# Softmax over heads: GpSimd adds the two halves of the heads in two of five units

## The reference, cut to what matters

```python
q = (Query @ Wq.T).reshape(b, -1, H, DK).transpose(0, 2, 1, 3)
k = (Key @ Wk.T).reshape(b, -1, H, DK).transpose(0, 2, 1, 3)
v = (Value @ Wv.T).reshape(b, -1, H, DK).transpose(0, 2, 1, 3)
scores = jnp.einsum('bhqd,bhkd->bhqk', q, k) / jnp.sqrt(jnp.float32(DK))
attn = jax.nn.softmax(scores, axis=1)
ctx = jnp.einsum('bhqk,bhkd->bhqd', attn, v)
ctx = ctx.transpose(0, 2, 1, 3).reshape(b, -1, H * DK)
return ctx @ Wo.T
```

## Time and profile before

| | |
|---|---|
| time, median of 3 runs | 1636.36 us (1632.52 to 1644.97) |
| the profiled execution, its own time | 1630.4 us |
| its span, first to last instruction | 1628.7 us |
| mean granted TensorE clock | 0.916 of full speed |
| busy: PE, DVE, ACT, POOL | 1406.0, 987.6, 687.7, 628.2 us |

### The profile page before, as it was taken

How to read it: one execution, slowest core, us unless ns; L and a number is a source line. 1 busy time by engine, 2 the same in 40 slices (tenths; PEclk the granted TensorE clock), 3 DMA queues, 4 the chain that set the end, 5 groups by cost and what they waited for, 6 DMA issues and landing times. The chain is left out here.

```text
span 1628.7 us, 23696 instructions
## 1 busy us (share of the span) xinstructions
PE 1406.0 (86%) x9145; PEld 715.1 (44%) x9145; DVE 987.6 (61%) x1770; ACT 687.7 (42%) x1204; POOL 628.2 (39%) x626
## 2 busy tenths in 40 slices
PE   7868786988989999899868999899999877889984
PEld 3345443433334444444334444454445433355542
DVE  4898939777742211468566773745556344588866
ACT  2444432766742000257534774244434432355522
POOL 2487734354223221333124312533421312356762
PEclk8889997989999999879987998999999978999996
DMA  5000010000020000100001002000000010000000
GB/s 111 0 1 0 1 48 1 1 1 1 1 82 1 1 0 0 53 1 1 11 0 54 2 2 47 1 2 1 2 1 2 2 31 1 7 1 2 2 1 28
DMA packets 17382, 20.65 MB, mean 13 GB/s; under 512 B 7835, under 2 KB 13195, under 8 KB 16760
## 3 DMA queue, kind: packets, MB, share of 16 engines
q1 hardware_dynamic: 15440, 17.33, 3.6%
q10 hardware_dynamic: 1832, 1.80, 0.5%
HBM read 17.94 MB, written 1.05 MB: 12 GB/s over the span
## 5 line engine op out<-in xcount | busy, mean ns | idle before, releaser
L1852 DVE CUSTOM_DVE_ANT_0 P<-P,L2f_mask 128x128 f32<-128x128 f32 (+3 forms) x256 | 118.5, 521 | 99.9 <-PE P L1744 99.9
L1029 DVE TENSOR_REDUCE L0f_nm<-P 128x2 f32<-128x768 f32 (+3 forms) x88 | 97.5, 1120 | 38.1 <-PE P L926 37.9
L2028 PE MATMUL P<-L0m_hm,L0m_w 128*128 128x512 f32 x256 | 112.2, 597 | 0.0
L1822 ACT ACTIVATE L2f_prob<-P 128x1024 f32<-128x1024 f32 x80 | 80.6, 1025 | 73.1 <-PE P L1756 73.1
L1663 POOL TENSOR_SCALAR_AFFINE_SELECT L2f_prob<-L2f_prob 128x512 f32<-128x512 f32 x64 | 39.9, 638 | 161.4 <-ACT L2f_prob L1822 161.4
L983 ACT ACTIVATE L0f_prob<-P 128x512 f32<-128x512 f32 x160 | 86.9, 610 | 33.8 <-PE P L937 32.5
L1744 PE MATMUL P<-L2f_ks,L2f_qs 48*128 48x512 f32 (+3 forms) x512 | 90.9, 467 | 0.3 <-DVE L2f_nm L1852 0.3
L1756 PE MATMUL P<-L2f_qs,L2f_ks 49*128 49x256 f32 (+3 forms) x512 | 84.5, 444 | 3.1 <-DVE L2f_nm L1852 2.3
L2431 POOL TENSOR_TENSOR L3x_exm<-L3x_exm,L3x_rec 128x2048 f32<-128x2048 f32 x16 | 72.4, 4530 | 24.1 <-DVE L3x_rec L2617 24.1
L1306 PE MATMUL P<-ident,L0x_pv 128*128 128x128 f32 x384 | 53.7, 305 | 27.1 <-POOL L0x_pv L1207 27.1
L880 POOL TENSOR_SCALAR_AFFINE_SELECT L0f_prob<-L0f_prob 128x512 f32<-128x512 f32 x64 | 39.9, 638 | 95.2 <-ACT L0f_prob L983 88.3
(11 more groups left out here) (578 smaller groups left out, 3329.5 us busy)
## 6 DMA issues: line engine op xcount, KB each, us to landing
L0m_w<-in_L0m_w SPq DMA_DIRECT2D x1, 2048.0 KB, 8.0
L0f_va<-in_L0f_va SPq DMA_DIRECT2D x3, 512.0 KB, 5.3
L0x_prod<-in_x SPq DMA_DIRECT2D x2, 512.0 KB, 5.9
L0x_segi<-in_segb SPq DMA_DIRECT2D x1, 1024.0 KB, 18.2
L0m_w<-in_L0m_w SPq DMA_DIRECT2D x1, 1024.0 KB, 10.0
out<-out_o SPq DMA_DIRECT2D x4, 256.0 KB, 2.4
L1x_va<-in_va SPq DMA_DIRECT2D x3, 256.0 KB, 3.1
L1x_vr<-in_vr SPq DMA_DIRECT2D x3, 256.0 KB, 4.1
```

Of the source, the lines that this page charges most:

```text
L1029: nc.vector.tensor_reduce(S.nm[:, qt, first:first + 2 * many].rearrange("p (i e) -> p e i", e=2), P[:, bank:bank + 2, 0:many * width].rear ...
L1822: nc.scalar.activation(S.prob_of(b, g)[:, at:at + 2, :], P[:, bank:bank + 2, :], ACT.Exp).then_inc(*S.act_done.up())
L1852: m = nc.vector.tensor_tensor_reduce(out=at, in0=at, in1=mask[:, T - width:T], scale=1.0, scalar=-3.0e38, op0=ALU.add, op1=ALU.max, accum_ ...
L2028: m = mm(P[:, slot(b, i) + part, :], w1[:, e, part * 512 + i * 128:part * 512 + i * 128 + 128], hm[b % 2][:, e, :], start=e == 0, stop=e = ...
```

## The change

In units 2 and 4 of each batch (`ADDED`) GpSimd adds heads 8 to 15 of the exponentials to heads 0 to 7 (128 x 1024) into one of two new tiles, `two`. TensorE's sum of such a unit then takes two products of the identity with that tile, in place of four with the exponentials, and waits for the addition in place of the exponentials. The other three units stay as they are. In the list two steps are added: `a2` right behind `e2`, and `a4` right behind `e4`. On POOL this makes the order

```diff
+    ADDED = (2, 4)
...
+        self.two = [sb(f"two{i}", [128, 8, 128]) for i in range(2)]
+        self.added = c("added")
...
-STEP_over_order = """... n2 S2 e2 m2 tk0 r2 q2 tk1 on t2 m3 w0 e3 S3 w3 w1 t3 e4 w2 out r3 v3 m4 n3 r4 res S4 t4 v4 n4""".split()
+STEP_over_order = """... n2 S2 e2 a2 m2 tk0 r2 q2 tk1 on t2 m3 w0 e3 S3 w3 w1 t3 e4 a4 w2 out r3 v3 m4 n3 r4 res S4 t4 v4 n4""".split()
...
+                elif kind == "add":
+                    pool.wait_ge(S.exp_done.sem, 10 * b + 2 * n + 2)
+                    i = 2 * b + S.ADDED.index(n)
+                    if i > 1:
+                        pool.wait_ge(S.sum_full.sem, 5 * (b - 1) + n + 1)
+                    ex = S.ex_of(b, n)
+                    nc.gpsimd.tensor_tensor(S.two[i % 2][:], half(ex, 0), half(ex, 1), ALU.add).then_inc(*S.added.up())
...
-                    for e in range(2):
+                    if n in S.ADDED:
+                        at = 2 * b + S.ADDED.index(n)
+                        pe.wait_ge(S.added.sem, at + 1)
+                        for i in range(2):
+                            m = mm(P[:, 4, :], G["ident"][:], S.two[at % 2][:, 4 * i:4 * i + 4, :].rearrange("p h q -> p (h q)"),
+                                   start=i == 0, stop=i == 1)
+                    for e in range(0 if n in S.ADDED else 2):
```

More of the change, by code:

```diff
@@ L2360, in terms @@
         return (self.xq, self.xqr) if who == "q" else (self.xk, self.xkr), [[term(c) for c in cs] for cs in (hi, mid, lo)]
-STEP_over_order = """q m0 n0 k1 r0 kv S0 t0 n1 v0 S1 t1 e0 q0 e1 q1 v1 m1 r1 k0 k2 n2 S2 e2 m2 tk0 r2 q2 tk1 on t2 m3 w0 e3 S3 w3 w1 t3 e4 w2 out r3 v3 m4 n3 r4 res S4 t4 v4 n4""".split()
+STEP_over_order = """q m0 n0 k1 r0 kv S0 t0 n1 v0 S1 t1 e0 q0 e1 q1 v1 m1 r1 k0 k2 n2 S2 e2 a2 m2 tk0 r2 q2 tk1 on t2 m3 w0 e3 S3 w3 w1 t3 e4 a4 w2 out r3 v3 m4 n3 r4 res S4 t4 v4 n4""".split()
 def over_order(STEP=STEP_over_order):
@@ L2377, in one @@
             return (kind, b - 1, 0) if b else None
-        kind, back = {"S": ("scores", 1), "m": ("max", 0), "e": ("exp", 0), "r": ("rec", -1), "n": ("norm", -1), "t": ("sum", 0),
+        kind, back = {"S": ("scores", 1), "m": ("max", 0), "e": ("exp", 0), "a": ("add", 0), "r": ("rec", -1), "n": ("norm", -1), "t": ("sum", 0),
                       "v": ("values", -2)}[kind]
```

## The result

The changed kernel takes 1665.17 us (median of 4 runs, 1662.75 to 1676.92) against 1636.76 before (four runs): a ratio of 1.0182, 95% interval 1.0118 to 1.0245. 1674 was forecast, with a range of 1658 to 1690.

What follows compares the result with a forecast made beforehand. PE was taken as the bound, with POOL nearly full in the stage; 28.8 us from POOL's order plus 9 for the clock gave 37.8 on the median of 1636.4, so 1674 us, range 1658 to 1690.

Steps and rivals of the forecast that it cites:

- PE's waits before sum 2: On PE, sum 2 waits for POOL's addition queued behind norm 1: 9.0, 7.9, 8.1 and 6.8 us later in batches 0 to 3.
- A batch's period: Time from sum 4 to sum 4 on PE: some 45 us instead of 37.6.
- The price of an addition: One 128 x 1024 addition on POOL: 2.28 us, bounds 2.2 and 2.55.
- the semaphore: Between the end of POOL's addition and the start of sum 2 on PE: 0.05 us.
- Norm 2 behind `a4`: In POOL's queue norm 2 follows `a4`, so values 2 wait about 1.9 us and sum 4's 1.8 us saving is lost.
- The wait of POOL ahead of `a4`: POOL stands some 9 us before each `a4`, released by the exponentials.
- The clock: PE at half clock after waits before sum 2: 1.7 to 2.8 us each, 7 to 11 in all, 9 taken.
- the 28.8 worked out at full clock: Delay of the whole stage from POOL's order, without clock cost: 8.1 + 5.1 + 6.5 + 9.1 us over four batches.
- all seven waits: Skill's stronger clock rule: each of seven PE waits in the stage pays 1.7 us, 12 us in place of 9.
- the walk of the prediction: Queue order followed through each batch at full clock: values 2 later by 8.1, 5.1, 6.5 us; batch 3's last norm by 9.1.
- the first rival: Additions done before PE asks: all eight sums keep their 1.8 us, about -14, 1622 us; chance 4%.
- The second rival: The wait is paid once, later stretches making up the shift: 8 + 9 less saved sums, about +12, 1648 us; chance 7%.

Runs made afterwards that it cites:

- experiment 1: Changed kernel, but the eight GpSimd additions are made and not used: TensorE takes all four products and doesn't wait for an addition; 1641.92 us, 1.0052 of before.
- 4: Changed kernel with `a2` ahead of the queries' split and norm 1, and `a4` behind norm 2, in GpSimd's queue; 1640.04 us, 1.0042 of before.
- experiment 5: Changed kernel with all eight additions on VectorE, behind the inverses of units 1 and 3; 1634.64 us, 0.9975 of before.
- experiment 6: Changed kernel with only unit 4 added up, on GpSimd, `a4` behind norm 2; 1628.21 us, 0.9952 of before.
- experiment 3: Changed kernel with 34 (batch 3: 28) dummy products on TensorE ahead of the wait for unit 2's addition; 1668.15 us, 1.0212 of before.
- experiment 8: Changed kernel once more, no edit, for a second profile; 1677.44 us (2 runs), 1.0235 of before.
- 7: Changed kernel with unit 2 added up on VectorE and unit 4 on GpSimd behind norm 2; 1633.95 us, 0.9962 of before.
- 9: Changed kernel with only unit 4 added up, on GpSimd, `a4` ahead of norm 2; 1649.40 us, 1.0075 of before.

## Why the prediction was right

**PE's waits before sum 2.** Forecast delays of 9.0, 7.9, 8.1 and 6.8 us; measured waits 8.69, 8.11, 8.14 and 6.91. A batch's period, from sum 4 to sum 4, became 45.9 us (1511.89 to 1557.77), some 45 forecast. The mechanism is shown: with the additions unused (1) or elsewhere (4) these waits are gone, or 1.9 us at most, and so is most of the loss.

**The price of an addition.** 2.28 us estimated, 2.35 measured, inside the bounds of 2.2 and 2.55. (On VectorE the same addition took 1.16 us in experiment 5.) The 0.05 us that the prediction gave the semaphore had no row; from the end of the addition to the start of sum 2 it is 0.15 us (1543.72 to 1543.87).

**Norm 2 behind `a4`.** A wait of 1.9 us before values 2 was forecast for batch 2; 1.90 measured, in the others 2.43, 1.91 and, in the last, 2.41. That this wait takes the whole gain of sum 4 is shown by the rows (3.89 us from sum 4 to values 2 in batch 1, 3.63 before) and by experiment 6, where the wait is gone and the gain is there. The wait of POOL ahead of `a4` was forecast too short, some 9 us against 11.05 to 11.73: with sum 2 at half clock the exponentials of unit 4 come later still.

**The clock.** 7 to 11 us, 9 taken; the stage lost 10.1 us beyond the 28.8 worked out at full clock. Sum 2 took 3.49 to 3.75 us, 3.6 forecast: 6.8 us in the four sums, and experiment 3 gives 6.0 back, while another wait lost the clock instead. That the total fits as well as it does is in part luck. The rest of the 9 stood for w0 and scores 4 behind sum 2, which were at half clock in batches 1 and 3 alone (in batch 1 0.75 us longer together). In their place came stretches at half clock that the 9 left out: sum 0 behind values 2 of batch 2 (4.99 us, before 3.70), sum 3 of batch 3 (5.31, before 3.70), and 0.75 us ahead of the first sum. The Trainium skill's stronger form (TensorE: Matmul & The Clock Gate, HAM oscillation), a fall in every turn of the loop, holds for the four waits before sum 2; of the waits before values 2 in the changed kernel, those of batches 0 and 1 passed without one (the projections behind them took 1.16 us), the ones of batches 2 and 3 did not (a sum of 4.99 us, values of 1.93). The loop that the Trainium skill describes there stands longer than these 1.9 to 2.4 us in each turn, so the prediction stretched the rule when it counted all seven waits.

**The batches.** How much later values 2 start than before, counted from the first scores, less the batches ahead; the forecast is the walk of the prediction and a quarter of its 9 us for the clock:

| | forecast | measured |
|---|---|---|
| batch 0 | 8.1 + 2.25 = 10.4 | 10.6 |
| batch 1 | 5.1 + 2.25 = 7.4 | 7.5 |
| batch 2 | 6.5 + 2.25 = 8.8 | 8.2 |
| batch 3, to the last product | 9.1 + 2.25 = 11.4 | 12.6 |
| stage | 37.8 | 38.9 |

Of batch 0's 10.6, 0.75 us lie ahead of its first sum, where the clock was at half for longer than before; every run with the two new tiles starts its stage at half clock (first scores 1.46 us, before 0.91), also experiment 1, and why is open. The program's median moved by 28 us in the first four runs and by 42 in the two of experiment 8; the stage's 38.9 lies between. The forecast of 1674 is thus off mainly by the stages that the change doesn't touch.

**What was wrong in it** is the first rival's price. It said that additions done in time would let all eight sums keep their 1.8 us, 14 us in all. Experiment 5 did that, on VectorE, in all eight sums but one; the program's time did not move beyond its interval, and the stage was 5.3 us longer. Sum 2's gain runs into the wait for the queries' terms or is lost to the clock, and a part of that wait comes from VectorE's slowing of GpSimd; only sum 4 has nothing late behind it (6); and the clock takes back what is left. The second rival's sum is off too: 8 + 9 less the four shortened sums of two batches, 7.2, is about 10 and not 12.

**Left open**: why the clock falls in one kernel and not in another at the same place, as at the sum of unit 2 in batch 2 of experiment 6, where no wait stands ahead; and where the lower median of experiment 6 comes from. In experiments 5 and 7, too, the program is not slower although the stage is 5.3 and 3.8 us longer, so small differences in the program's time say little of this stage.

## What to carry to other kernels

Before giving a step to an engine with idle time, look at which instruction of that engine stands ahead of it in its queue when the result is wanted: POOL was 39% busy in the program, and had no gap in the 14 us that mattered. Look also at what is queued behind a step that has to wait; `a4` held up a ready norm. And price a saving by what is late next: of two shortened sums one was worth 1.7 us, and the other ran into the next wait.

## What the runs showed of the hardware

The clock of TensorE in this stage repeats with the kernel: in each of three kernels that were profiled twice, both executions show the same sums at half clock (5.16 and 5.17, 3.75 and 3.75, 4.99 and 4.97, 5.31 and 5.30 us in the change). Falls came at waits of 0.6 to 2 us in some places (4, 9), a wait of 1.9 passed without one in others, and at the sum of unit 2 the clock also fell while TensorE had been working without a pause (batches 1 and 2 of experiment 6, batch 1 of the kernel before). So a short wait is not shown to be what lowers it.

An addition of two SBUF operands on VectorE and GpSimd's instructions slow each other, and the one that starts later pays (5, 7). The addition that started while a norm still ran took 1.76 us; the one that started 0.16 us ahead of a norm took 1.16, and the norm 5.38 instead of 4.52. A cast of GpSimd, with one operand, took 1.49 instead of 0.61 us beside an addition (7). The ends in batch 2 look as if they took turns: the norm ends at 1526.10, the addition 1.09 us behind it, and the split's first instruction (1.17 us before) 1.01 us behind that. VectorE's subtraction, with one operand in PSUM, shows no such thing: two of them take 2.35 us both beside a norm of GpSimd (at 1522.97 in the change) and while GpSimd stands (at 1424.55). The Trainium skill names the contention (GPSIMD Engine Reference, Key points: VectorE instructions with two SBUF inputs); this trace agrees.
